# Token choice: the expert outputs turned by VectorE in 32 by 32 blocks, in place of a round trip through memory

## The chip, the cores and the metric

One NeuronCore of a Trainium2 chip runs the whole program. The metric is the device time of one execution in microseconds. The kernel before takes 2503.06 us, the median of 3 runs (2500.81 to 2505.09).

## The reference, cut to what matters

The program is four layers, each with a residual and a layer norm: window attention, token choice, linear attention, nested width attention. The change is in token choice (8 sequences of 1024 tokens of 256 numbers; tokens in groups of 16; 64 experts):

```python
grouped = x.reshape(x.shape[:-2] + (-1, ne, d))                    # groups of 16 tokens
logits = jnp.einsum('...btd,des->...btes', grouped, controller) + tie
perm = (logits == jnp.max(logits, axis=-3, keepdims=True))         # each expert takes one token of a group
sel = jnp.einsum('...btd,...btes->...besd', grouped, perm)
inner = jax.nn.relu(jnp.einsum('...besd,desf->...besf', sel, f1) + bias)
inter = jnp.einsum('...besf,esfd->...besd', inner, f2)             # the expert outputs
out = jnp.einsum('...besd,...btes->...btd', inter, perm)           # back to the tokens
x = layernorm(x + out)
```

## The kernel before, in words

`token_choice_layer` (from L820) handles two sequences, so 128 groups, in a block; there are NB = 4 blocks X = 0 to 3. The 64 experts are done in two halves of 32. A half has these stages:

- **selection**: for 8 pairs of tiles, PE transposes the one-hot choice (`pT`, L1254), ACT copies it (`chosen`, L1125), PE multiplies it with the tokens (`sel`, L1263), and the result is copied from PSUM half by ACT (L1153), half by DVE (L1188) into `sel`, as 32 experts by 128 groups.
- **h**: the first expert weights, two steps of 64 matmuls (L1269), with a relu into `hidden` by ACT (L1161) and DVE (L1194, 8 instructions a step).
- **inter**: the second expert weights, 8 steps of 8 matmuls (L1276). ACT (L1165) and DVE (L1199) copy the result into `wide`: partition = group, then 32 experts by 256 numbers. These are the expert outputs.
- **out**: back to the tokens, 4 steps of 16 matmuls (L1283), whose weights must have the partition run over 4 groups by 32 experts, which is not how `wide` stands after `inter`. DVE adds each result to `x` (L1209) and in the second half takes layer norm statistics (L176, L182).

Between `inter` and `out` the array is re-laid through memory: after each `inter` step SP stores 512 KB to `expert_outputs` (L1062, 8 a half), and the step `gather` loads the whole half back in four pieces of 1 MB in the other layout (L1076). `out` waits for its piece (`back`, L1244).

The order of all engines comes from one list `steps` (L856 to L863), each step with a block offset. The out steps of a half stand after the selection and the first `h` step of the next half, so the round trip has that time to hide in. The **early half** is `out` of half 0 of a block, behind the selection of half 1; on PE the transposes of the next block's tokens (`xT`, L957), their copies (L975) and `logits` (L969) follow it. The **late half** is `out` of half 1, behind the selection of the next block's half 0. After the last block nothing stands in front of it but the round trip; its end is called the **tail** here, with the linear attention layer's opening (weights loaded by ACT's queue, L1423 to L1429, once `wide` is free, and PE at L1549 and L1561). PSUM has four slots that steps use in turn, so `out` step 0 frees the slot of the fifth step after.

SP's queue carries the expert stores, the loads back, the next block's tokens (L1056), the second weights f2 (L1070) and the results (L1080), in the order of the list.

Of the kernel before, what the change touches and what calls it, by code (L numbers as in the profile page):

```python
# [819 lines left out]
def token_choice_layer(nc, block, semaphores, kept, x_in, y_out, controller, f1_in, f2_in, f1_bias, tie_in, ident_in, scratch):  # L820
# [35 lines left out]
    steps = [(-1, "gather", 1), (0, "f2", 2), (0, "f2", 3)] + s[2:] + e[:1] + late + [(-1, "aggregate", 0), (0, "spread", 1)]  # L856
    steps += e[1:4] + [(0, "f2", 4), (-1, "rescale", 0), e[4], (-1, "rescale", 1), e[5], (0, "f2", 5), (-1, "rescale", 2), e[6],
                       (-1, "rescale", 3), e[7], turned[0], e[8], turned[1], e[9]]
    steps += [(-1, "store", 1), (-1, "store", 0), (0, "gather", 0), (1, "load", 0), (1, "load", 1), (0, "f2", 6), (0, "f2", 7)]
    s, e, early = selection(1), experts(1), combination(0, 0)  # L860
    steps += s[2:] + e[:1] + early + [(1, "xT", n) for n in range(4)] + [(1, "logits", 0), (1, "second", 0)]
# [26 lines left out]
    def signal(name, per, step=1):  # L888
        return Signal(sem(name), per, step)
# [13 lines left out]
    left = [signal(f"left{half}", IN, 16) for half in range(2)]  # L903
    normed = [signal(f"normed{n}", NT) for n in range(2)]
    back = [signal(f"back{i}", 2, 16) for i in range(NC)]
# [71 lines left out]
    class First:  # L977
# [12 lines left out]
        def start_sp(self, sp):  # L990
            for s in (*f2_loaded, *x_loaded, *stored, *left, *back):
                s.start(sp)
# [49 lines left out]
    def programs(tail, sb, ps):  # L1042
        sel = sb("sel", [P, CH, EH, NG])
        schedule.slots = [ps(f"slot{i}", [P, 1024]) for i in range(4)]

        @block.sync
        def _(sp):
            def piece(step, X, seq, n, B):
# [8 lines left out]
                if kind == "inter":  # L1057
                    half, n = divmod(i, IN)
                    inter_even.wait(sp, X, i + 1)
                    alone(sp)  # L1060
                    inter_odd.wait(sp, X, i + 1)
                    left[half].by(sp.dma_start(scratch[half, :, 4 * n:4 * n + 4, :], wide[:, 4 * n:4 * n + 4, :]))  # L1062
# [54 lines left out]
        def _(act):  # L1117
# [9 lines left out]
            def piece(step, X, seq, n, B):  # L1127
# [42 lines left out]
        def _(dve):  # L1170
            def piece(step, X, seq, n, B):
# [11 lines left out]
                if kind == "sel":  # L1183
                    tp = i % TP
                    s = arrived(dve, X, step)[:, 512:1024].rearrange("p (g e) -> p e g", e=EH)
                    if tp == 0:
                        schedule.wait_filled(dve, X if i else X - 1, ("h", 1 if i else 3))
                    sel_odd.by(dve.tensor_copy(sel[:, 1, :, 16 * tp:16 * tp + 16], s))  # L1188
# [28 lines left out]
        def _(pe):  # L1217
# [6 lines left out]
            def piece(step, X, seq, n, B):  # L1224
# [18 lines left out]
                if kind == "out":  # L1243
                    back[i % NC].wait(pe, X, i // NC + 1)  # L1244
# [33 lines left out]
                if kind == "out":  # L1278
# [12 lines left out]
                    [(b.sem, b.count(NB - 1)) for b in back], schedule.left())  # L1291
# [834 lines left out]
def four_layers(nc, x, wq, wk, bq, bk, wv, bv, wo, bo, cos, sin, mask, maskT, ident, ident16,  # L2126
# [80 lines left out]
```

How the kernel before makes its waits and increments, by code:

```python
def wait_alone(eng, sem, value):  # L63
    eng.wait_ge(sem, value)
    alone(eng)
# [37 lines left out]
    def wait(self, eng, block, n=None):  # L103
        eng.wait_ge(self.sem, self.count(block, n))
# [27 lines left out]
    def wait_free(self, pe, b, key):  # L133
        old = self.before(key)
        if old is not None:
            for sem, per_sequence, position in self.emptied(old):
                pe.wait_ge(sem, b * per_sequence + position)
# [44 lines left out]
    def reciprocal_root(self, pool, b, use):  # L184
        pool.wait_ge(self.aggregated, self.count(b, use) * self.tiles)
        pool.tensor_scalar(self.mv[:, :, 1], self.mv[:, :, 1], LN_EPS, None, ALU.add).then_inc(self.var_ready, 1)
        pool.wait_ge(self.var_ready, self.count(b, use))
        pool.tensor_tensor(self.rstd[:, :], self.mv[:, :, 1], self.half[:, :], ALU.pow).then_inc(self.rstd_ready, 1)
# [45 lines left out]
    def wait_memsets(self, eng):  # L235
        eng.wait_ge(self.setup, 3)
# [15 lines left out]
def negative_mean(pool, ln, to, sems, X):  # L252
    pool.wait_ge(ln.rstd_ready, X + 1)
    pool.tensor_tensor(to[:, :], ln.mv[:, :, 0], ln.rstd[:, :], ALU.mult).then_inc(sems[0], 1)
    pool.wait_ge(sems[0], X + 1)
    pool.tensor_scalar(to[:, :], to[:, :], -1.0, None, ALU.mult).then_inc(sems[1], 1)
# [43 lines left out]
    def use(self, pe, X, step, B):  # L301
# [5 lines left out]
        if i > -4 * size:  # L307
            for sem, count in self.until(B + i // size, self.plan[i % size]):
                pe.wait_ge(sem, count)
        return self.slot_in(B, step)
# [649 lines left out]
    def logits(pe, X, s):  # L960
        if X == 0:
            pe.wait_ge(consts, 16 * NCONST)
        xT_even.wait(pe, X)
```

## Time and profile before

| | us |
|---|---|
| median of 3 runs | 2503.06 |
| lowest, highest | 2500.81, 2505.09 |
| the profiled execution's own time | 2499.96 |
| its span | 2498.1 |
| mean granted TensorE clock | 0.966 of full speed |
| busy: PE, DVE, ACT, POOL | 2175.6, 1420.4, 996.3, 901.0 |

The profiled execution is 3.1 us under the median of the runs. The token choice layer's matmuls run from about 1054 to 1438 us of the span. In the timelines a row is a start, a length, an engine, a line, an operation, out and in, and a count; in brackets stands the engine's idle time just before and what ended it.

### The profile page before, as it was taken

The numbers are of one execution on the slowest core, as the hardware profiler recorded it, in microseconds if no ns is written. First come the engines' busy times: TensorE is split into PE (matmuls) and PEld (weight loads), VectorE is DVE, ScalarE is ACT, GpSimd is POOL, SyncE is SP. The second block draws the span as 40 slices with busy tenths as digits, with TensorE's granted clock in tenths as the row PEclk, the third lists the DMA queues.
The fourth block names the chain that finished last, engine by engine and source line by source line (L and its number), as shares of the span: only waits on it lengthen the run. The fifth ranks groups of instructions, "written<-read, shape, count | busy, mean of one in ns | idle before, by whom it ended". The sixth has DMA issues, their size and how long they took to land.

```text
span 2498.1 us, 42625 instructions
## 1 busy us (share of the span) xinstructions
PE 2175.6 (87%) x17140; PEld 1362.6 (55%) x17140; DVE 1420.4 (57%) x2526; ACT 996.3 (40%) x1450; POOL 901.0 (36%) x573
## 2 busy tenths in 40 slices
PE   4899999999999999888878699999688888888885
PEld 2445555555555555566656556775455555555553
DVE  3545555555555555546566435544467777677772
ACT  1233333333333333444535243334245554555443
POOL 4222222222222220203123022101448877787784
PEclk7899999999999999999999899999789999999997
DMA  6555555555555554376796832101654465445511
GB/s 146 124 109 116 116 112 111 111 111 111 111 111 111 111 103 69 129 245 236 267 306 219 288 123 68 49 19 51 181 140 116 109 179 137 139 111 155 130 35 51
DMA packets 228355, 328.81 MB, mean 132 GB/s; under 512 B 14928, under 2 KB 167488, under 8 KB 227904
## 3 DMA queue, kind: packets, MB, share of 16 engines
q1 hardware_dynamic: 221168, 321.49, 49.2%
q10 hardware_dynamic: 6992, 4.60, 0.7%
q8 instruction: 137, 2.24, 0.4%
q14 instruction: 58, 0.48, 0.1%
HBM read 197.46 MB, written 127.93 MB: 130 GB/s over the span
## 4 chain that ended last, share of the span: by engine, by line
PE 57%; DVE 17%; DMA 7%; POOL 6%; ACT 6%; issue 3%; SPq 3%; ACTq 1%; DVEq 0%; POOLq 0%
PE l0a_slot L775 8%; PE l0a_slot L785 7%; PE l0a_O L710 6%; DVE l1f_rowmax L1978 5%; PE l1a_slot L1570 4%; PE l0a_slot L752 4%; POOL l1f_added L1855 3%; DMA l0f_wide<-expert_outputs 2%; PE l0a_slot L757 2%; ACT l0f_f L590 2%; PE l1a_slot L1561 2%; DMA expert_outputs<-l0f_wide 2%; PE l0a_slot L803 2%; DVE l0f_hidden L655 2%; PE l1a_slot L1612 2%
## 5 line engine op out<-in xcount | busy, mean ns | idle before, releaser
L590 ACT ACTIVATE l0f_f<-l0a_slot 128x1024 f32<-128x1024 f32 (+1 forms) x256 | 248.6, 972 | 339.0 <-PE l0a_slot L775 189.2
L655 DVE TENSOR_REDUCE l0f_hidden<-l0a_slot 128x4 f32<-128x1024 f32 (+1 forms) x256 | 293.5, 1156 | 114.2 <-PE l0a_slot L785 111.2
L1927 ACT ACTIVATE l1f_probs<-l1f_slot 128x1024 f32<-128x1024 f32 x240 | 244.1, 1023 | 251.0 <-PE l1f_slot L2109 245.7
L1978 DVE TENSOR_REDUCE l1f_rowmax<-l1f_slot 128x1 f32<-128x1024 f32 x240 | 287.5, 1217 | 70.1 <-PE l1f_slot L2100 69.7
L1855 POOL TENSOR_TENSOR l1f_added<-l1f_probs 128x1024 f32<-128x1024 f32 x117 | 277.4, 2371 | 133.1 <-ACT l1f_probs L1927 125.3
L775 PE MATMUL l0a_slot<-l0f_hidden 128*128 128x512 bf16 (+1 forms) x1024 | 296.0, 374 | 13.5 <-DMA l0f_hl<-qk_rows 9.1
L549 POOL TENSOR_TENSOR l0f_x<-l0f_x 128x512 f32<-128x512 f32 x32 | 40.8, 1274 | 538.6 <-DVE l0f_x L639 538.6
L2109 PE MATMUL l1f_slot<-l1f_Qs,l1f_Ks 128*128 128x256 f32 x960 | 171.5, 302 | 37.7 <-DVE l1f_lo L1968 14.8
L2100 PE MATMUL l1f_slot<-l1f_Ks,l1f_Qs 96*128 96x512 f32 x480 | 173.7, 447 | 26.0 <-DVE l1f_rowmax L1978 19.9
L2109 PEld LDWEIGHTS l1f_slot<-l1f_Qs,l1f_Ks 128*128 128x128 f32 x960 | 144.1, 194 | 93.1 <-DVE l1f_rowmax L1978 29.8
L710 PE MATMUL l0a_O<-l0f_f,l0f_wide 128*32 128x128 f32 x3840 | 156.1, 279 | 9.4 <-issue 9.4
L1857 POOL TENSOR_TENSOR l1f_added<-l1f_added 128x512 f32<-128x512 f32 x117 | 150.0, 1282 | 9.2
L2033 PE MATMUL l1f_os<-l1f_probs,l1f_V 128*32 128x256 f32 x1920 | 143.5, 392 | 0.1
L785 PE MATMUL l0a_slot<-l0a_Qs,l0f_hl 49*128 49x256 f32 (+1 forms) x1024 | 127.3, 327 | 18.3 <-ACT l0f_f L590 17.1
L785 PEld LDWEIGHTS l0a_slot<-l0f_hl,l0a_Qs 48*128 48x128 f32 x1024 | 77.7, 188 | 103.8 <-issue 103.8
L785 PEld LDWEIGHTS l0a_slot<-l0a_Qs,l0f_hl 49*128 49x128 f32 x1024 | 76.8, 186 | 103.4 <-issue 68.4
L785 PE MATMUL l0a_slot<-l0f_hl,l0a_Qs 48*128 48x256 f32 (+1 forms) x1024 | 128.7, 330 | 0.0
L752 PE MATMUL l0a_slot<-l0f_x,l0f_spread 128*128 128x512 f32 x256 | 123.1, 627 | 6.3 <-DVE l0f_spread L623 4.8
L710 PEld LDWEIGHTS l0a_O<-l0f_f,l0f_wide 128*32 128x32 f32 x3840 | 90.2, 109 | 63.3 <-issue 36.1
L775 PEld LDWEIGHTS l0a_slot<-l0f_hidden 128*128 128x128 bf16 x1024 | 63.8, 97 | 97.0 <-issue 62.3
L2100 PEld LDWEIGHTS l1f_slot<-l1f_Ks,l1f_Qs 96*128 96x128 f32 x480 | 76.9, 196 | 71.8 <-issue 30.9
L601 ACT COPY l0f_f<-l0a_O 128x512 f32<-128x512 f32 x64 | 37.5, 585 | 194.8 <-PE l0a_O L710 194.6
(194 smaller groups left out, 3750.3 us busy)
## 6 DMA issues: line engine op xcount, KB each, us to landing
expert_outputs<-l0f_wide SPq DMA_DIRECT2D x64, 512.0 KB, 5.3
l0f_wide<-expert_outputs SPq DMA_DIRECT2D x32, 1024.0 KB, 11.5
l1f_Ks<-kq_rows SPq DMA_DIRECT2D x48, 512.0 KB, 8.7
l0a_Qs<-qk_rows SPq DMA_DIRECT2D x90, 256.0 KB, 7.9
l0f_hl<-qk_rows SPq DMA_DIRECT2D x90, 256.0 KB, 14.9
qk_rows<-l0f_wide SPq DMA_DIRECT2D x32, 512.0 KB, 2.8
qk_rows<-l0f_x SPq DMA_DIRECT2D x32, 512.0 KB, 4.1
l0f_f<-in_dram SPq DMA_DIRECT2D x32, 512.0 KB, 7.7
```

Of the source, the lines that this page charges most:

```text
L590: exp_ready.by(act.activation(probs[:, t % 2, HG * g:HG * g + HG, 0:reach, :], s[:, :, 0:reach, :], ACT.Exp, scale=SCALE))
L655: max_ready.by(dve.reduce_max(rowmax[:, t, :, 2 * g:2 * g + 2], s[:, :, :, first:2 * P], AX))
L710: last = mm(O[t % 2][32 * j:32 * j + 32, g, :], V[:, tile - a, HG * g + j, :], probs[:, (t - a) % 2, HG * g + 2 * (j % 2) + j // 2, a, :], ...
L752: last = mm(s[:, BW * r:BW * r + BW], w[:, c, P * r:P * r + P], xT[:, n, c, :], start=c == 0, stop=c == CH - 1)
L775: at_end = mm(o[:, half, :, reach, :], ident16[:, :], table[:, reach, :].unsqueeze(1).broadcast_to([P, 2, wide, P]), start=not mask_ends, ...
L785: last = mm(o[:, half, j, reach, :].rearrange("p a q -> p (a q)"), left[r, 2 * g + j, here], right[r, 2 * g + j, moving], start=mask_ends ...
L1855: halved.by(pool.tensor_tensor(added[:, u, :], probs[:, 0, u, :], probs[:, 1, u, :], ALU.add))
L1857: add_done.by(pool.tensor_tensor(added[:, u, 0:SKT * QW], added[:, u, 0:SKT * QW], added[:, u, SKT * QW:HKT * QW], ALU.add))
L1927: exp_done.by(act.activation(probs[:, half, u - FIRST[b], :], s[:, :], ACT.Exp, scale=SCALE))
L1978: max_done.by(dve.reduce_max(rowmax[:, i:i + 1], s[:, :], AX))
L2100: last = mm(s[:, 512 * half:512 * half + 512], Qs[0:96, parity, u, P * t:P * t + P], Ks[0:96, parity, UNITS[u][0], 512 * half:512 * half + ...
L2109: last = mm(s[:, QW * j:QW * j + QW], Ks[:, parity, UNITS[u][0], P * kt:P * kt + P], Qs[:, parity, u, :], start=True, stop=True)
```

## The change

The stores of the expert outputs, the loads back and the scratch in memory go, with their semaphores `left` and `back`. In their place DVE turns `wide` in place: 8 instructions a half (`turn`, NTURN = 8), each over 128 partitions and 32 of the 256 columns by 32 experts; seen as partition, column, expert, every block of 32 partitions by 32 experts is transposed. An instruction reads and writes its 1024 numbers a partition with a step of 256 numbers, 1 KB. For the blocks to hold what `out` needs, the selection copies write the groups as (4 residues, 32 quads) and no longer as (32 quads, 4 residues): runs of 4 numbers where there were runs of 16. The turns are merged into the list among the selection steps of the next half. `out` waits for all 8 turns of its half. The linear attention layer's first loads wait for the last turn where they waited for the last load back.

```diff
+    NTURN = 8
+    def turns(offset, half):
+        return [(offset, "turn", NTURN * half + n) for n in range(NTURN)]
-    steps = [(-1, "gather", 1), (0, "f2", 2), (0, "f2", 3)] + s[2:] + e[:1] + late + [(-1, "aggregate", 0), (0, "spread", 1)]
+    steps = [(0, "f2", 2), (0, "f2", 3)] + merged(s[2:], turns(-1, 1)) + e[:1] + late + [(-1, "aggregate", 0), (0, "spread", 1)]
...
-    steps += [(-1, "store", 1), (-1, "store", 0), (0, "gather", 0), (1, "load", 0), (1, "load", 1), (0, "f2", 6), (0, "f2", 7)]
+    steps += [(-1, "store", 1), (-1, "store", 0), (1, "load", 0), (1, "load", 1), (0, "f2", 6), (0, "f2", 7)]
...
-    steps += s[2:] + e[:1] + early + [(1, "xT", n) for n in range(4)] + [(1, "logits", 0), (1, "second", 0)]
+    steps += merged(s[2:], turns(0, 0)) + e[:1] + early + [(1, "xT", n) for n in range(4)] + [(1, "logits", 0), (1, "second", 0)]
...
+        by_quad = sel[:, :, :, :].rearrange("p c e (j q) -> p c e j q", j=J)
+        by_word = wide[:, :, :].rearrange("p e d -> p d e")
-                if kind == "inter":
-                    left[half].by(sp.dma_start(scratch[half, :, 4 * n:4 * n + 4, :], wide[:, 4 * n:4 * n + 4, :]))
-                if kind == "gather":
-                    wait_alone(sp, left[i].sem, (X + 3) * IN * 16)
-                    rows = scratch[i, :, :, :].rearrange("(q j) e d -> (j e) q d", j=J)
-                    for n in range(NC):
-                        q = slice(NQ // NC * n, NQ // NC * (n + 1))
-                        back[n].by(sp.dma_start(wide[:, q, :], rows[:, q, :]))
-                    sel_odd.by(dve.tensor_copy(sel[:, 1, :, 16 * tp:16 * tp + 16], s))
+                    sel_odd.by(dve.tensor_copy(by_quad[:, 1, :, :, 4 * tp:4 * tp + 4], s))
+                if kind == "turn":
+                    half, n = divmod(i, NTURN)
+                    if n == 0:
+                        inter_even.wait(dve, X, IN * half + IN)
+                        inter_odd.wait(dve, X, IN * half + IN)
+                    part = by_word[:, D // NTURN * n:D // NTURN * (n + 1), :]
+                    turned_round.by(dve.transpose(part, part))
-                    back[i % NC].wait(pe, X, i // NC + 1)
+                    turned_round.wait(pe, X, NTURN * (i // NC + 1))
-                    [(b.sem, b.count(NB - 1)) for b in back], schedule.left())
+                    [(turned_round.sem, turned_round.count(NB - 1))], schedule.left())
```

On DVE, from the inter copies (`l0f_wide`) of half 0 to its late selection copies (`l0f_sel`), the order before:

```order
L1199 COPY l0f_wide<-l0f_slot 128x2x256 x2
L1194 TENSOR_SCALAR l0f_hidden<-l0f_slot,l0f_b 64x128 x8
L1199 COPY l0f_wide<-l0f_slot 128x2x256 x6
L1188 COPY l0f_sel<-l0f_slot 128x32x16 x8
L1194 TENSOR_SCALAR l0f_hidden<-l0f_slot,l0f_b 64x128 x8
```

At the same place now, down to the third selection copy:

```order
L1193 COPY l0f_wide<-l0f_slot 128x2x256 x2
L1188 TENSOR_SCALAR l0f_hidden<-l0f_slot,l0f_b 64x128 x8
L1193 COPY l0f_wide<-l0f_slot 128x2x256 x6
L1182 COPY l0f_sel<-l0f_slot 128x128x4
L1200 STREAM_TRANSPOSE l0f_wide<-l0f_wide 128x32x32
L1182 COPY l0f_sel<-l0f_slot 128x128x4
L1200 STREAM_TRANSPOSE l0f_wide<-l0f_wide 128x32x32 x2
L1182 COPY l0f_sel<-l0f_slot 128x128x4
```

Eight turns stand among the eight selection copies, one for one on the whole, and the last copy comes after the last turn.

On SP's queue, one half's stores and the steps behind them to the next block's tokens (`l0f_x<-x`), before:

```order
L1062 DMA expert_outputs<-l0f_wide 128x1024 x2
L1070 DMA l0f_f<-in_dram 128x4x256
L1062 DMA expert_outputs<-l0f_wide 128x1024 x4
L1080 DMA x<-l0f_x 128x8x256 x2
L1076 DMA l0f_wide<-expert_outputs 128x8x256 x4
L1056 DMA l0f_x<-x 128x8x256 x2
```

and now, from the weights (`l0f_f`) of a block on:

```order
L1062 DMA l0f_x<-x 128x8x256 x2
L1070 DMA l0f_f<-in_dram 128x4x256 x8
L1074 DMA x<-l0f_x 128x8x256 x2
L1062 DMA l0f_x<-x 128x8x256 x2
L1070 DMA l0f_f<-in_dram 128x4x256 x8
```

The loads of the next tokens stand right behind the stores of the block before.

## Rows read from the trace of the kernel before

**Rows 1.** The page: its head, and the chain that ended last by line.

```profile
span 2498.1 us, 42625 instructions
PE l0a_slot L775 8%; PE l0a_slot L785 7%; PE l0a_O L710 6%; DVE l1f_rowmax L1978 5%; PE l1a_slot L1570 4%; PE l0a_slot L752 4%; POOL l1f_added L1855 3%; DMA l0f_wide<-expert_outputs 2%; PE l0a_slot L757 2%; ACT l0f_f L590 2%; PE l1a_slot L1561 2%; DMA expert_outputs<-l0f_wide 2%; PE l0a_slot L803 2%; DVE l0f_hidden L655 2%; PE l1a_slot L1612 2%
```

**Rows 2.** Waits, 1054 to 1450 us: total us, times, longest us.

```profile
PE l0f_slot L1283 <- DMA l0f_wide<-expert_outputs: 43.2, 25, 12.2
PE l0f_slot L957 <- DMA l0f_x<-x: 6.7, 6, 1.2
```

**Rows 3.** Timeline of PE, the second block's early half.

```profile
1184.65 1.81 PE L1263 MATMUL l0f_slot<-l0f_chosen,l0f_hl 128*128 128x256 f32 x8
...
1186.44 1.20 PE L1263 MATMUL l0f_slot<-l0f_chosen,l0f_hl 128*128 128x256 f32 x8
...
1200.09 1.95 PE L1283 MATMUL l0f_slot<-l0f_wide,l0f_spread 128*64 128x256 f32 x16
1203.34 1.95 PE L1283 MATMUL l0f_slot<-l0f_wide,l0f_spread 128*64 128x256 f32 x16 [1.31 <-DMA l0f_wide<-expert_outputs]
...
1209.37 1.95 PE L1283 MATMUL l0f_slot<-l0f_wide,l0f_spread 128*64 128x256 f32 x16 [1.06 <-DMA l0f_wide<-expert_outputs]
1212.47 1.94 PE L957 MATMUL l0f_slot<-l0f_ident,l0f_x 128*128 128x128 f32 x16 [1.16 <-DMA l0f_x<-x]
...
1218.83 3.64 PE L969 MATMUL l0f_slot<-l0f_wide,l0f_ctrl 128*32 128x512 f32 x32 [1.41 <-DVE l0f_wide L975]
```

**Rows 4.** Timeline of SP's queue, there.

```profile
1191.70 8.50 SPq L1076 DMA_DIRECT2D l0f_wide<-expert_outputs  x4
1200.30 6.00 SPq L1056 DMA_DIRECT2D l0f_x<-x  x2
```

**Rows 5.** Timeline of DVE, the second block's late half.

```profile
1236.55 0.69 DVE L1188 COPY l0f_sel<-l0f_slot 128x512 f32<-128x512 f32 x1 [0.44 <-PE l0f_slot L1263]
...
1245.46 0.69 DVE L1188 COPY l0f_sel<-l0f_slot 128x512 f32<-128x512 f32 x1 [0.58 <-PE l0f_slot L1263]
1250.12 2.26 DVE L1194 TENSOR_SCALAR l0f_hidden<-l0f_slot,l0f_b 64x128 f32<-64x128 f32 x8 [3.96 <-PE l0f_slot L1269]
...
1253.81 1.40 DVE L176 BATCH_NORM_STATS2 l0f_ln_stats<-l0f_x 128x6 f32<-128x256 f32 x4
...
1265.92 1.17 DVE L182 BATCH_NORM_AGGREGATE l0f_ln_mv<-l0f_ln_stats 128x2 f32<-128x6 f32 x16
1267.00 1.26 DVE L1199 COPY l0f_wide<-l0f_slot 128x512 f32<-128x512 f32 x2
```

**Rows 6.** The chain that ended last, 1410 to 1480 us: start us, us, what.

```profile
1414.62 5.40 DMA expert_outputs<-l0f_wide
...
1435.97 0.38 ACTq L1423
...
1440.73 7.86 DMA l1a_head_blocks<-in_dram
...
1448.64 14.00 PE l1a_slot L1561 x32
```

**Rows 7.** Timeline of PE, the tail.

```profile
1442.15 5.27 PE L1549 MATMUL l1a_slot<-opening_ident,l1a_x 128*128 128x128 f32 x32 [4.37 <-issue]
```

**Rows 8.** Groups of DVE by shape: busy us, mean ns, idle before.

```profile
L1209 DVE TENSOR_TENSOR l0f_x<-l0f_slot,l0f_x 128x1024 f32<-128x1024 f32 x32 | 39.1, 1223 | 46.1 <-PE l0f_slot L1283 45.8
...
L195 DVE TENSOR_SCALAR l1a_y<-l1a_sum,l1a_ln_mv,l1a_ln_rstd 128x256 f32<-128x256 f32 x64 | 21.1, 406 | 0.0
...
L1959 DVE TENSOR_SCALAR l1f_xT<-l1f_slot,l1f_nw,l1f_nb 128x256 f32<-128x256 f32 x7 | 3.7, 535 | 0.0
```

**Rows 9.** Line L623 alone: duration ns least, median, most; first and last start.

```profile
L623 DVE COPY l0f_spread<-l0f_x x4: 361/367/6516, 8.7 to 15.7; 128x256 f32<-128x256 f32 x4
```

**Rows 10.** Stretches: length, engines' busy us, granted TensorE clock, DMA share, GB/s.

```profile
1235.00:1246.00 11.00, 10.36 (x80) 9.19 (x76) 6.07 (x9) 9.22 (x22) 0.68 (x1) 1.00 0.80 305
1263.00:1280.00 17.00, 14.98 (x135) 11.24 (x134) 14.31 (x45) 7.68 (x20) 12.10 (x12) 0.85 0.61 208
```

More of the change, by code:

```diff
@@ L817, in window_attention_layer, with token_choice_layer @@
                     spent=[(signal.sem, signal.step, signal.count(NBLOCK - 1)) for signal in spent])
-def token_choice_layer(nc, block, semaphores, kept, x_in, y_out, controller, f1_in, f2_in, f1_bias, tie_in, ident_in, scratch):
+def token_choice_layer(nc, block, semaphores, kept, x_in, y_out, controller, f1_in, f2_in, f1_bias, tie_in, ident_in):
     G = 16
@@ L902, in token_choice_layer @@
     inter_even = signal("inter_even", 2 * IN); inter_odd = signal("inter_odd", 2 * IN)
-    left = [signal(f"left{half}", IN, 16) for half in range(2)]
+    turned_round = signal("turned_round", 2 * NTURN)
     normed = [signal(f"normed{n}", NT) for n in range(2)]
-    back = [signal(f"back{i}", 2, 16) for i in range(NC)]
     summed = signal("summed", 2 * NC)
@@ L990, in start_sp @@
         def start_sp(self, sp):
-            for s in (*f2_loaded, *x_loaded, *stored, *left, *back):
+            for s in (*f2_loaded, *x_loaded, *stored):
                 s.start(sp)
@@ L1002, in start_dve @@
         def start_dve(self, dve):
-            for s in (xT_odd, rated, best_ready, choice_ready, lo_ready[0], normed[1], sel_odd, hidden_odd, inter_odd, summed):
+            for s in (xT_odd, rated, best_ready, choice_ready, lo_ready[0], normed[1], sel_odd, hidden_odd, inter_odd, turned_round, summed):
                 s.start(dve)
@@ L1056, in piece @@
                     x_loaded[i].by(sp.dma_start(x[:, X % 2, part, :], tokens(x_in, 2 * X + i)))
-                if kind == "inter":
[L1058 to L1061, printed above, removed]
-                    left[half].by(sp.dma_start(scratch[half, :, 4 * n:4 * n + 4, :], wide[:, 4 * n:4 * n + 4, :]))
                 if kind == "f2":
@@ L1149, in piece @@
                     tp = i % TP
-                    s = arrived(act, X, step)[:, 0:512].rearrange("p (g e) -> p e g", e=EH)
+                    s = arrived(act, X, step)[:, 0:512].rearrange("p (q j e) -> p e j q", q=4, j=J)
                     if tp == 0:
                         schedule.wait_filled(act, X if i else X - 1, ("h", 1 if i else 3))
-                    sel_even.by(act.copy(sel[:, 0, :, 16 * tp:16 * tp + 16], s))
+                    sel_even.by(act.copy(by_quad[:, 0, :, :, 4 * tp:4 * tp + 4], s))
                 if kind == "h":
@@ L1184, in piece @@
                     tp = i % TP
[L1185 removed]
+                    s = arrived(dve, X, step)[:, 512:1024].rearrange("p (q j e) -> p e j q", q=4, j=J)
                     if tp == 0:
                         schedule.wait_filled(dve, X if i else X - 1, ("h", 1 if i else 3))
[L1188 removed]
+                    sel_odd.by(dve.tensor_copy(by_quad[:, 1, :, :, 4 * tp:4 * tp + 4], s))
                 if kind == "h":
@@ L2137, in four_layers @@
             with ExitStack() as kept:
-                first, programs = token_choice_layer(nc, block, semaphores, kept, x1, x2, controller, f1, f2, f1_bias, tie, ident,
-                                                     dram("expert_outputs", (2, 128, 32, D)))
+                first, programs = token_choice_layer(nc, block, semaphores, kept, x1, x2, controller, f1, f2, f1_bias, tie, ident)
                 tail = window_attention_layer(nc, block, semaphores, x, x1, wq, wk, bq, bk, wv, bv, wo, bo, cos, sin, mask, maskT, ident,
```

## The prediction

> **What bounds the kernel now.** I read the page first: of a span of 2498.1 us the chain that ended last passes, with 2% each, through the stores of the expert outputs and through the loads back [rows 1]. So the round trip that the change removes is on the path. Next the waits inside the token choice layer: PE stood 43.2 us for pieces loaded back, in 25 waits, and 6.7 us for the next block's tokens [rows 2]. That is the most that can be won, 50 us, if what replaces the trip costs nothing. The timelines then tell what else fills those places.
>
> In the early half [rows 3], out steps that take PE 1.95 us start 3.0 us apart, each after a wait for its piece (1.31, then 1.06 twice), and the tokens come late too, since their loads stand on SP's queue behind the loads back, which took 8.5 us to issue [rows 4]. In the late half [rows 5] DVE paces the selection no more than PE does: eight copies of 0.69 us start 1.27 us apart (8.91 us from the first start to the last), so DVE is idle 0.58 us before each. That idle time, 8 x 0.58 = 4.6 us a half, is all the cover there is for the turns. Behind it DVE is the tighter engine: hidden 2.26 us, then adds with statistics, then the aggregate, and the inter copies start at 1267.00, without a pause.
>
> **What a turn costs.** No row shows a transpose by DVE, nor an instruction whose every number lies 1 KB from the last, on its input and its output. Bounds come from three rows.
> - Lower end: the add of 1024 numbers takes 1.223 us [rows 8] and the copy of 512 takes 0.69 [rows 5], so 1.04 ns a number and 0.16 us fixed. At that rate a turn takes 1.22 us. No row of DVE that reads 1024 numbers is below it.
> - A row with steps: L623 copies 256 numbers that lie 16 numbers apart, SBUF to SBUF, in 0.361 to 0.367 us; the one of 6.5 us is left aside, POOL was filling memory then [rows 9]. Such instructions go two numbers at a time: 256 numbers with two scalars take 535 ns from PSUM and 406 from SBUF, 129 ns less, which is half of 256 x 1.04 [rows 8]. Without steps L623 would take 128 x 1.04 + 160 = 0.29 us. It took (364 - 160) / 128 = 1.6 ns for each pair in place of 1.04. I read the 0.58 ns as the price of a read that never stays in place. A turn that pays it once a number takes 1024 x 1.62 + 160 = 1.82 us.
> - Upper end: the turn writes with the same step, and if the write pays as much on top, 1024 x 2.2 + 160 = 2.41 us.
>
> I take **2.0 us**, nearer to 1.82: the add of rows 8 reads two streams and writes one at the plain rate, so reads and writes run side by side and their prices should overlap in part.
>
> The Trainium skill (Vector Engine (DVE) Microarchitecture Reference, section 5.2, Measured stream behaviour on trn2) gives 1.73 ns a column for one input that hops at each element, 1.71 for an output that does, and 1.98 for all three streams. By it a turn would take an estimated 1.85 to 2.1 us, and the sum below would be 33 to 49 us before the clock's term. L623 agrees with its direction (1.6 ns); that the price falls on a transpose no run here shows.
>
> **The sum, by the length T of a turn.** Back to back, two copies of 0.69 take 1.26 us [rows 5], so each instruction overlaps the one before by about 0.1.
> - Selection, in the 7 halves that have one behind them (the tail has none): before, first copy to the end of the last 9.6 us. Now DVE alone sets it: 8 x (0.59 + T - 0.1) + 0.1 = 8T + 4.0. That is **8T - 5.6** longer. PE has its four slots ahead and ACT is not moved, so neither waits longer than DVE does; h, and out behind it, start later by that much.
> - Early half, blocks 0 to 2: from the first out to logits 18.74 us [rows 3]. Without the waits PE needs 4 x 1.95 + 2 x 1.94 + the 1.41 for the last token copy, 13.1. The tokens are no cause any more: their loads issue once the stores before them have landed, some 15 us before they are wanted. **5.6 won**, net 8T - 11.2, three times.
> - Early half, block 3: no tokens follow, so only the waits between outs go, 1.31 + 1.06 + 1.06 = **3.4**; net 8T - 9.0.
> - Late half, blocks 0 to 2: DVE's aggregate ended 16.97 us after hidden started [rows 5]. Without waits it is 2.26 + 4 x (1.23 + 1.40) + 1.17 = 13.95, DVE being the limit there and no longer the loads. **3.0 won**, net 8T - 8.6, three times.
> - Tail: from the last store to L1561 of the next layer 34.0 us [rows 6]. Now eight turns with nothing beside them, 8T - 0.8, then out 1.95, four adds and three statistics 9.1 until the slots are free, and 6.5 from L1549 to L1561 [rows 6, 7]: 8T + 16.8. The next layer's weights need 12.6 us from their first issue [rows 6] and may start at the last turn: hidden. Net **8T - 17.2**.
>
> Together 3(8T - 11.2) + (8T - 9.0) + 3(8T - 8.6) + (8T - 17.2) = **64T - 85.6**. It is zero at T = 1.34. At 1.22 it is -7.5, at 1.82 +31, at 2.0 **+42**, at 2.41 +69.
>
> Other edits: 64 MB of transfers less cost the engines nothing and the waits for them are counted. The selection copies write runs of 4 numbers where they wrote 16; runs of 16 ran at the plain rate (0.69 us), and I leave that, with the idle ACT as cover. The f2 loads issue earlier and nobody waited for them.
>
> TensorE's clock: the granted clock was 1.00 in 1235 to 1246 us, where PE was busy 10.4 of 11 us, and 0.85 in 1263 to 1280, where it waited between its steps [rows 10]; right after that a selection step took 1.81 us, and the next 1.20 [rows 3]. With a slower DVE, PE will have a gap at each selection step, and h behind it may start at the lower level (1.2 of 2.4 GHz). I put 0.6 us on each of 7 halves, **+4**.
>
> Sum +46.6 on the profiled execution's own 2499.96 us: 2546.6; that execution lies 3.1 us under the median of the runs, so I forecast **2550 us** for a median.
>
> **Rivals.**
> 1. **The turns run at the plain rate** (T = 1.22 to 1.30), and the kernel is faster or the same. The mechanism is the idle 0.58 us in front of each selection copy plus the waits removed behind it; the tail alone then gives 7. It decides below T = 1.34. For it: the copies from PSUM with a step of 32 numbers take 0.69 us, as those without [rows 5]. Against: those read PSUM, and the only stepped read of SBUF, L623, pays. -7.5 to -2.4, so 2496 to 2501. Chance 0.17. The Trainium skill (same page, section 3.8, The reshape front-end and per-opcode configuration) says that the transposing array is pipelined to one element a cycle a lane, which is this rival; it speaks of the array, not of the streams that feed it, and nothing in the trace before shows it.
> 2. **A part of the price** (T = 1.35 to 1.75): -1 to +26 before the clock, 2502 to 2533. Chance 0.08.
> 3. **Reads and writes both pay in full, or PE runs h at the lower clock.** T = 2.41 gives +69, with the clock +73: 2576. Or T = 2.0 and h at half speed in 7 halves: 7 x 3.7 (its length, within the 3.96 us that DVE waits for it [rows 5]) = +26 in place of +4: 2571. Both: 2598. Chance 0.18, of it 0.03 above 2592.
> 4. The change does not do what it says: were a piece of the trip left, PE would still wait for it; the order on SP's queue shows none left. No chance of its own.
>
> **How the numbers follow.** The forecast (T = 1.75 to 2.35, clock term 0 to 8) has 0.57. The range starts inside rival 2 at 2515 and ends at 2592: left out are rival 1 (0.17) and 0.03 above. What a measurement of this kernel can tell from no change is about 0.2%, 5 us. Faster by more than that: the lower part of rival 1 with the clock unchanged, 0.11. Within it: the rest of rival 1 (0.06) and the start of rival 2 (0.02), 0.08. Slower: 0.81.
>
> **What would show it.** In the profile after, the line of the transpose has 64 instructions with a mean near 2.0 us, so DVE gains some 125 us of busy time. In a selection stage DVE has no idle time, copies start about 2.5 us apart, and PE waits there for DVE's `l0f_sel`. Out steps start 1.95 us apart in the early half, no wait for a load stands in front of them, and logits come some 5 us later after the selection's start than before. From the last inter copy to L1561 it is about 33 us. DMA moves 64 MB less. The prediction is wrong if the transpose's mean is near 1.2 us, or if it is near 2 us and the sum is still near zero: then PE or the round trip, not DVE, set the selection.

## The result, and the profile after

The changed kernel takes 2560.22 us (median of 4 runs, 2555.83 to 2564.27), beside 2501.93 us of the kernel before on the same chip: ratio 1.0232, 95% interval 1.0211 to 1.0254. It is slower. The forecast was 2550 us in a range of 2515 to 2592. The profiled execution took 2559.29 us, 59.3 us more than that of before.

The page after: span, engines, transfers, and the chain by line, to be held against [rows 1].

```profile
span 2557.4 us, 42521 instructions
PE 2199.7 (86%) x17140; PEld 1393.3 (54%) x17140; DVE 1548.7 (61%) x2590; ACT 996.5 (39%) x1450; POOL 900.7 (35%) x573
DMA packets 185859, 261.69 MB, mean 102 GB/s; under 512 B 13392, under 2 KB 133184, under 8 KB 185408
PE l0a_slot L775 8%; PE l0a_slot L785 7%; PE l0a_O L710 5%; DVE l0f_wide L1200 5%; DVE l1f_rowmax L1979 5%; PE l1a_slot L1571 4%; PE l0a_slot L752 4%; POOL l1f_added L1856 3%; PE l0a_slot L757 2%; ACT l0f_f L590 2%; PE l1a_slot L1613 2%; PE l1a_slot L1562 2%; PE l0a_slot L803 2%; DVE l0f_hidden L655 2%; PE l0f_slot L1270 2%
```

Both pieces of the round trip are gone from the chain. The turns (L1200) stand in it with 5%, and h (L1270) has come in. DVE is busy 128.3 us more, PE 24.1 us more although it has the same matmuls. The transfers fell by 67.1 MB, from the 328.81 MB on the page of before.

The groups of DVE by shape (busy us, mean ns of one, idle before):

```profile
L1200 DVE STREAM_TRANSPOSE l0f_wide<-l0f_wide 128x1024 f32<-128x1024 f32 x64 | 141.4, 2232 | 0.2
...
L1182 DVE COPY l0f_sel<-l0f_slot 128x512 f32<-128x512 f32 x64 | 42.6, 667 | 10.8 <-PE l0f_slot L1264 10.8
```

A turn takes 2.23 us, between the 2.0 that the forecast took and its upper end of 2.41. The selection copies with their runs of 4 numbers cost nothing (0.67 us).

Waits of PE from 1054 to 1500 us (total, times, longest), against [rows 2]:

```profile
PE l0f_slot L1270 <- DVE l0f_sel L1182: 39.4, 8, 6.0
PE l0f_slot L1264 <- DVE l0f_sel L1182: 32.0, 15, 3.4
PE l0f_slot L1284 <- DVE l0f_wide L1200: 17.3, 1, 17.3
```

No wait for a load is left. PE now waits for DVE's selection copies, in front of h above all, and once, in the tail, for the turns.

Timelines of the second block's early half: DVE, then PE. The counterparts are [rows 5] for the copies (of the late half) and [rows 3] for PE.

```profile
1203.12 0.69 DVE L1182 COPY l0f_sel<-l0f_slot 128x512 f32<-128x512 f32 x1 [1.31 <-PE l0f_slot L1264]
1203.73 2.32 DVE L1200 STREAM_TRANSPOSE l0f_wide<-l0f_wide 128x1024 f32<-128x1024 f32 x1
1205.94 0.65 DVE L1182 COPY l0f_sel<-l0f_slot 128x512 f32<-128x512 f32 x1
...
1222.12 2.16 DVE L1200 STREAM_TRANSPOSE l0f_wide<-l0f_wide 128x1024 f32<-128x1024 f32 x1
1224.19 0.64 DVE L1182 COPY l0f_sel<-l0f_slot 128x512 f32<-128x512 f32 x1
1230.47 2.26 DVE L1188 TENSOR_SCALAR l0f_hidden<-l0f_slot,l0f_b 64x128 f32<-64x128 f32 x8 [5.64 <-PE l0f_slot L1270]
```

```profile
1211.51 2.04 PE L1264 MATMUL l0f_slot<-l0f_chosen,l0f_hl 128*128 128x256 f32 x8 [3.36 <-DVE l0f_sel L1182]
...
1225.03 5.40 PE L1270 MATMUL l0f_slot<-l0f_sel,l0f_f 128*64 128x128 f32 x64 [5.34 <-DVE l0f_sel L1182]
1230.25 7.09 PE L1284 MATMUL l0f_slot<-l0f_wide,l0f_spread 128*64 128x256 f32 x64
1237.27 3.71 PE L961 MATMUL l0f_slot<-l0f_ident,l0f_x 128*128 128x128 f32 x32
1242.39 3.64 PE L973 MATMUL l0f_slot<-l0f_wide,l0f_ctrl 128*32 128x512 f32 x32 [1.41 <-DVE l0f_wide L979]
```

From the first copy to the end of the last it is 21.7 us, without a gap on DVE behind the first copy. The last turn ends at 1224.28 and h starts at 1225.03, so no turn runs beside h. DVE stands still for 5.64 us while h runs. On PE the 64 matmuls of out follow each other without a wait, and from out to logits it is 12.1 us where it was 18.7. But h takes 5.40 us where the same 64 matmuls took 3.71 before. The next stretch (length, engines' busy us, granted clock, DMA share, GB/s), which begins just before h, shows why:

```profile
1224.00:1237.00 13.00, 11.97 (x128) 10.06 (x128) 6.70 (x13) 2.14 (x8) 0.00 (x0) 0.83 0.00 1
1475.00:1492.00 17.00, 0.00 (x0) 0.00 (x0) 16.89 (x9) 0.45 (x1) 0.00 (x0) 0.58 0.00 0
1492.00:1502.00 10.00, 9.85 (x64) 5.76 (x64) 5.86 (x12) 0.00 (x0) 0.00 (x0) 0.69 0.79 265
```

PE was busy nearly all of the 13 us at a granted clock of 0.83, a mean of the levels 1.2 and 2.4 GHz, behind a wait of 5.34 us. The tail shows it harder: 17 us without a matmul at 0.58, then out at 0.69, in 10.09 us where it took 7.09 in the middle.

The late half of the same block, DVE:

```profile
1281.50 0.64 DVE L1182 COPY l0f_sel<-l0f_slot 128x512 f32<-128x512 f32 x1
1288.13 2.26 DVE L1188 TENSOR_SCALAR l0f_hidden<-l0f_slot,l0f_b 64x128 f32<-64x128 f32 x8 [5.99 <-PE l0f_slot L1270]
...
1300.88 1.17 DVE L182 BATCH_NORM_AGGREGATE l0f_ln_mv<-l0f_ln_stats 128x2 f32<-128x6 f32 x16
```

From hidden to the end of the aggregate it is 13.92 us; the prediction had 13.95.

The chain that ended last, tail:

```profile
1474.86 0.70 DVE l0f_wide L1193
...
1475.66 0.30 DVE l0f_wide L1200
1475.96 1.78 issue
1477.74 14.36 DVE l0f_wide L1200 x7
...
1492.15 6.66 PE l0f_slot L1284 x32
...
1507.27 13.73 PE l1a_slot L1562 x32
```

On this chain 31.7 us lie between the end of the last inter copy (1475.56) and L1562, where before 34.0 us lay between the start of the last store's transfer and the same step [rows 6].

### The profile page after: what moved, and what is told of

It reads as the page before. It is cut to its first block, busy times and chain, and to the rows that moved or that the text cites. A ratio compares the mean times of both kernels' runs of the same rounds, so it can differ in the third digit from the quotient of the medians.

```text
span 2557.4 us, 42521 instructions
## 1 busy us (share of the span) xinstructions
PE 2199.7 (86%) x17140; PEld 1393.3 (54%) x17140; DVE 1548.7 (61%) x2590; ACT 996.5 (39%) x1450; POOL 900.7 (35%) x573
## 4 chain that ended last, share of the span: by engine, by line
PE 58%; DVE 24%; POOL 6%; ACT 5%; issue 3%; DMA 1%; ACTq 1%; SPq 0%; DVEq 0%; POOLq 0%
PE l0a_slot L775 8%; PE l0a_slot L785 7%; PE l0a_O L710 5%; DVE l0f_wide L1200 5%; DVE l1f_rowmax L1979 5%; PE l1a_slot L1571 4%; PE l0a_slot L752 4%; POOL l1f_added L1856 3%; PE l0a_slot L757 2%; ACT l0f_f L590 2%; PE l1a_slot L1613 2%; PE l1a_slot L1562 2%; PE l0a_slot L803 2%; DVE l0f_hidden L655 2%; PE l0f_slot L1270 2%
## 5 line engine op out<-in xcount | busy, mean ns | idle before, releaser
L775 PE MATMUL l0a_slot<-l0f_hidden 128*128 128x512 bf16 (+1 forms) x1024 | 296.1, 374 | 13.8 <-DMA l0f_hl<-qk_rows 9.4
L1200 DVE STREAM_TRANSPOSE l0f_wide<-l0f_wide 128x1024 f32<-128x1024 f32 x64 | 141.4, 2232 | 0.2
L1264 PE MATMUL l0f_slot<-l0f_chosen,l0f_hl 128*128 128x256 f32 x512 | 96.0, 346 | 37.3 <-DVE l0f_sel L1182 32.0
```

Of the source, the lines that this page charges most:

```text
L775: at_end = mm(o[:, half, :, reach, :], ident16[:, :], table[:, reach, :].unsqueeze(1).broadcast_to([P, 2, wide, P]), start=not mask_ends, ...
L1200: turned_round.by(dve.transpose(part, part))
```

## The experiments

**Theory**: the 1 KB step makes a turn nearly twice as long, and DVE, with turns and selection copies one for one, sets the selection; that outweighs the round trip, whose waits really were on the path. **Rivals**: the transpose is slow by itself; or the trip was hidden anyway and something else grew.

**1. plain_turn: the same turns on numbers that lie side by side.**

```diff
-                    part = by_word[:, D // NTURN * n:D // NTURN * (n + 1), :]
+                    part = wide[:, 4 * n:4 * n + 4, :].rearrange("p e (a b) -> p (e a) b", b=32)
```

> Each of the 64 turns transposes 1024 numbers that lie side by side (4 experts by 256 columns) in place, so the output isn't the reference's; count, size and waits are those of the change. Theory (the 1 KB step is the price of a turn): a turn takes 1.15 to 1.3 us, and by 64T - 85.6 the time comes to 2490 to 2500 us, 2510 at most if h still starts at the lower clock. Rival (the transpose is slow whatever its addresses): a turn stays near 2.2 us and the time near 2560 us.

Measured: 2493.14 us, ratio to before 0.9974 (0.9962 to 0.9986). The group of turns:

```profile
L1200 DVE STREAM_TRANSPOSE l0f_wide<-l0f_wide 128x1024 f32<-128x1024 f32 x64 | 77.1, 1222 | 0.2
```

The theory holds, and the rival falls: the transpose itself goes at the plain rate, and the step alone costs 1.0 us a turn and some 65 us in the whole (ratio to before 0.9974 in place of 1.0232). 64T - 85.6 gives -7.4 at T = 1.222; against the 2499.73 us of before in this set it was -6.6. That this fits so well is in part luck: h is long here too, in five of seven halves (5.07 to 6.49 us, 9.1 us over 3.71 together), and the sum has no term for it.

**2. short_turn: each turn cut to one of its 32 columns.**

```diff
-                    part = by_word[:, D // NTURN * n:D // NTURN * (n + 1), :]
+                    part = by_word[:, D // NTURN * n:D // NTURN * n + 1, :]
```

> Each turn transposes one column of 32 experts in place of 32 columns, so 31 of 32 columns are left unturned: the round trip is gone and nearly nothing is put in its place. Theory (the waits for the trip were worth what the sum gives them: 3 x 5.6 + 3.4 + 3 x 3.0, and 16 in the tail): 45 us less than before, 2452 to 2460 us, turns of 0.1 to 0.2 us, h back at 3.7 us. Rival (the waits come back elsewhere, the trip was mostly hidden): 2485 to 2502 us.

Measured: 2447.57 us, ratio 0.9791 (0.9770 to 0.9812), so 52 us less than before (2499.73), 7 us more than the 45 expected and past the lower end of its range. A shortened turn took 0.24 us where 0.1 to 0.2 was expected. The selection of the block's late half took 9.6 us as before, and h took 3.71 us in all 16 places. The round trip was on the path, and its removal is worth more than the sum gave it, although the 64 short turns are still there.

**3. hops: eight kinds of instruction over 1024 numbers in place of the eight turns.**

```diff
+                    turned_round.wait(dve, X, NTURN * half + n)
+                        turned_round.by(dve.transpose(plain, plain))
+                        turned_round.by(dve.transpose(plain, step))
+                        turned_round.by(dve.transpose(step, plain))
+                        turned_round.by(dve.transpose(step, step))
+                        turned_round.by(dve.transpose(two, two))
+                        turned_round.by(dve.transpose(eight, eight))
+                        turned_round.by(dve.tensor_copy(step, step))
+                        turned_round.by(dve.tensor_copy(plain, plain))
```

(The output stands first; `step` is 1 KB between numbers, `two` 8 B, `eight` 32 B. Each line stands under an `if n == 0` to `if n == 7`, left out here.)

> The eight turns of a half become eight different instructions over 1024 numbers, each behind a wait for the one before (the output isn't the reference's): 0 transpose side by side; 1 write 1 KB steps, read side by side is 2, read 1 KB steps and write side by side... in order: n=1 writes side by side in, steps out as given by the code (out plain, in stepped: n=1; out stepped, in plain: n=2); 3 both stepped as in the change; 4 both with steps of 8 B; 5 both with steps of 32 B; 6 a copy with 1 KB steps on both; 7 a copy side by side. Theory (each stepped stream has its own price and the two overlap in part): 0 at 1.2 us, 1 and 2 at 1.7 to 1.9, 3 at 2.2, 6 as 3. Rival a (only reads pay): 1 at 2.2, 2 at 1.2. Rival b (only writes pay): the reverse. Rival c (the transpose itself): 0 to 3 all near 2.2, 6 below 1.9. If the size of the step matters, 4 and 5 lie below 3; else they equal it.

Measured: 2509.76 us in its one execution; it was run for its durations. Each line alone, in the order of the diff (duration ns least, median, most; first and last start):

```profile
L1206 DVE STREAM_TRANSPOSE l0f_wide<-l0f_wide x8: 1235/1245/1247, 1088.7 to 1432.5; 128x1024 f32<-128x1024 f32 x8
L1208 DVE STREAM_TRANSPOSE l0f_wide<-l0f_wide x8: 1899/1958/2020, 1090.4 to 1433.8; 128x1024 f32<-128x1024 f32 x8
L1210 DVE STREAM_TRANSPOSE l0f_wide<-l0f_wide x8: 1900/1903/1909, 1092.4 to 1435.7; 128x1024 f32<-128x1024 f32 x8
L1212 DVE STREAM_TRANSPOSE l0f_wide<-l0f_wide x8: 2175/2250/2278, 1094.7 to 1437.7; 128x1024 f32<-128x1024 f32 x8
L1214 DVE STREAM_TRANSPOSE l0f_wide<-l0f_wide x8: 1223/1242/1262, 1097.5 to 1439.9; 128x1024 f32<-128x1024 f32 x8
L1216 DVE STREAM_TRANSPOSE l0f_wide<-l0f_wide x8: 2032/2116/2132, 1099.2 to 1441.2; 128x1024 f32<-128x1024 f32 x8
L1218 DVE COPY l0f_wide<-l0f_wide x8: 1189/1244/1273, 1101.8 to 1443.2; 128x1024 f32<-128x1024 f32 x8
L1220 DVE COPY l0f_wide<-l0f_wide x8: 658/682/705, 1103.5 to 1444.5; 128x1024 f32<-128x1024 f32 x8
```

Read and write each pay about the same when alone: (1958 - 1245) / 1024 = 0.70 ns a number for the read, 0.64 for the write. Together they pay 0.98, not 1.34: they run side by side in part. A step of 8 B costs nothing, one of 32 B nearly as much as 1 KB. The reads and writes alone came a little above the 1.7 to 1.9 us expected (1.96 and 1.90), and one expectation missed clearly: the copy with 1 KB steps took 1.24 us, 0.55 ns a number over the plain copy and far below the turn. Whether a copy, whose input and output steps are alike here, walks the addresses in the order written, no run tells.

**4. pe_fill: PE's gaps in the selection filled.** Half of the matmuls of a selection step are done twice.

```diff
-                            for part in (hi, lo):
+                            for part in (hi, lo) + ((hi, lo) if c == 0 and (X or i >= TP) else ()):
```

> The changed kernel with PE's idle time in the selections filled: 4 of the 8 matmuls of a selection step run twice (not in the very first selection). PE waits 2.0 us a step there less 0.6. Theory (h takes 5.2 to 6.1 us because PE had stood still in front of it and runs at the lower clock): h falls to 3.7 to 4.5 us and the time falls by 6 to 14 us, 2546 to 2554 us. Rival (the turns slow PE's reads, or the last wait of 5 us alone drops the clock): h stays at 5.2 to 6.1 us and the time is 2558 to 2565 us.

Measured: 2565.39 us (ratio to before 1.0255, 1.0227 to 1.0283), no better than the change. PE at h, two of seven halves:

```profile
1115.62 6.00 PE L1270 MATMUL l0f_slot<-l0f_sel,l0f_f 128*64 128x128 f32 x64 [5.07 <-DVE l0f_sel L1182]
...
1289.62 3.72 PE L1270 MATMUL l0f_slot<-l0f_sel,l0f_f 128*64 128x128 f32 x64 [3.71 <-DVE l0f_sel L1182]
```

A stretch inside each of these two (length, busy us of PE, PEld, DVE, ACT, POOL, granted clock, DMA share, GB/s):

```profile
1116.00:1121.00 5.00, 5.00 (x56) 5.00 (x54) 0.00 (x0) 0.00 (x0) 0.00 (x0) 0.57 0.01 3
1290.00:1293.00 3.00, 3.00 (x60) 3.00 (x58) 0.00 (x0) 0.00 (x0) 0.00 (x0) 1.00 0.02 5
```

So the clock makes h long, and not the turns' use of SBUF: in the slow stretch DVE does nothing at all, and PE goes through 56 matmuls in 5 us at 0.57 where it goes through 60 in 3 us at 1.00. Filling the gaps between the steps does not help. In six of seven halves one wait of 5.0 to 5.1 us stays in front of h, and h takes 5.1 to 6.5 us; only where that wait was 3.71 us did h take 3.72. The wait's length doesn't decide alone: plain_turn has an h of 3.71 us behind a wait of 3.09 us, columns_late one of 5.38 us behind 1.6 us. What decides in between, no run separates.

**5. late_two: the last two turns behind the last selection copy.**

```diff
-    merged(s[2:], turns(-1, 1)) + e[:1] + late
+    merged(s[2:], turns(-1, 1)[:6]) + turns(-1, 1)[6:] + e[:1] + late
```

(and the same in the early half.)

> The changed kernel with the last two of eight turns behind the last selection copy instead of among the copies. Theory (DVE alone sets the selection, and the 6 us for which it stands still while h runs are free cover): from the first selection copy to the last 17.7 us instead of 21.7, the two turns (4.4 us) lie beside h, the time falls by some 3.6 to 6 us in each of 7 halves, 2518 to 2535 us. Rival (the turns are only put off, out waits for them or the relu starts later by as much): 2552 to 2562 us.

Measured: 2525.58 us, ratio to before 1.0103 (1.0084 to 1.0122) in place of 1.0232, so some 32 us less than the change. DVE, the end of a late half:

```profile
1259.13 0.64 DVE L1182 COPY l0f_sel<-l0f_slot 128x512 f32<-128x512 f32 x1
1259.70 4.33 DVE L1200 STREAM_TRANSPOSE l0f_wide<-l0f_wide 128x1024 f32<-128x1024 f32 x2
1265.40 2.25 DVE L1188 TENSOR_SCALAR l0f_hidden<-l0f_slot,l0f_b 64x128 f32<-64x128 f32 x8 [1.37 <-PE l0f_slot L1270]
```

This selection began at 1242.01, so it took 17.8 us (expected 17.7). The two turns run in time in which DVE stood still. (h is still long in all seven halves, 5.0 to 5.4 us.) What costs is a turn **in front of a selection copy**, not a turn.

**6. act_sel: all selection copies on ACT.**

```diff
+                    s = slot[:, 512:1024].rearrange("p (q j e) -> p e j q", q=4, j=J)
+                    sel_odd.by(act.copy(by_quad[:, 1, :, :, 4 * tp:4 * tp + 4], s))
-                    sel_odd.by(dve.tensor_copy(by_quad[:, 1, :, :, 4 * tp:4 * tp + 4], s))
```

> The changed kernel with all selection copies on ACT, none on DVE. Theory (DVE's turns and copies together set the selection): 8 turns of 2.25 us alone, 17.5 to 18 us from the first turn, while ACT needs about 13.5 us; minus 4 us in each of 7 halves, plus some 3 us in the first selection, which has no turns: 2530 to 2540 us. Rival (PE, the slots or ACT set it as much as DVE): 2555 to 2570 us.

Measured: 2482.79 us, ratio 0.9939 (0.9923 to 0.9956): some 73 us less than the change by the ratios, and 15 us less than before (2498.04). The direction was expected, the size not. DVE and PE in the late half:

```profile
1226.49 17.29 DVE L1197 STREAM_TRANSPOSE l0f_wide<-l0f_wide 128x1024 f32<-128x1024 f32 x8
1243.81 2.26 DVE L1185 TENSOR_SCALAR l0f_hidden<-l0f_slot,l0f_b 64x128 f32<-64x128 f32 x8
```

```profile
1239.88 3.71 PE L1267 MATMUL l0f_slot<-l0f_sel,l0f_f 128*64 128x128 f32 x64 [1.32 <-ACT l0f_sel L1150]
1243.83 7.13 PE L1281 MATMUL l0f_slot<-l0f_wide,l0f_spread 128*64 128x256 f32 x64 [0.24 <-DVE l0f_wide L1197]
```

The expectation had still counted the turns into the selection. But h waits for the copies alone: it now starts 13.4 us after the first turn, runs beside the last turns at 3.71 us, and hidden and out follow the last turn at once. So the same 64 turns at nearly the same length (2270 ns in place of 2232) leave the kernel 58 us slower than before or 15 us faster, by what stands behind them on their engine. Of the 73 us between the two, 13.4 are h, which is short here.

**7 and 8. columns, columns_late: the array kept column by column**, the 32 experts of a column side by side; columns_late also puts three turns behind the last copy.

```diff
-        by_word = wide[:, :, :].rearrange("p e d -> p d e")
+        by_word = wide[:, :, :].rearrange("p e d -> p (e d)").rearrange("p (d e) -> p d e", e=EH)
+        by_expert = by_word.rearrange("p d e -> p e d")
-    act.copy(wide[:, e:e + 4:2, :], ...)
+    act.copy(by_expert[:, e:e + 4:2, :], ...)
```

(and likewise DVE's copy and out's `wide[:, q, :]`.)

> The array of the expert outputs is kept column by column, the 32 experts of a column side by side. The copies behind inter (ACT and DVE) write with steps of 128 B, the turns read and write side by side, out's matmuls read with steps of 128 B. Theory (a copy that works on one number at a time anyway pays nothing for a step, only the transpose does): copies stay at 0.69 us, turns at 1.22 us, and if PE's reads pay nothing either, the time is that of the side by side turns, 2488 to 2498 us. Rival (the price moves on to the copies or to out): each step of out twice as long would cost 7 us a half, 2545 to 2560 us; copies at 1.0 to 1.2 us would cost some 3 us a half, 2510 to 2520 us.

> As the run named columns, and the last three of eight turns behind the last selection copy. Theory: the selection takes 8 x 0.59 + 5 x 1.15 + 0.1 = 10.6 us, one more than without turns, and three turns (3.5 us) lie beside h: 7 us over the kernel with nothing in the trip's place in the halves, 8 us in the tail, 2458 to 2470 us. Rival (as for columns, out or the copies pay): 50 us more.

Measured: 2559.85 us (1.0254, 1.0236 to 1.0272) and 2534.10 us (1.0144, 1.0128 to 1.0159). Groups of columns:

```profile
L1201 DVE STREAM_TRANSPOSE l0f_wide<-l0f_wide 128x1024 f32<-128x1024 f32 x64 | 77.2, 1223 | 0.8 <-ACT l0f_wide L1160 0.7
L1194 DVE COPY l0f_wide<-l0f_slot 128x512 f32<-128x512 f32 x64 | 65.4, 1115 | 7.7 <-PE l0f_slot L1278 7.2
```

```profile
L1285 PE MATMUL l0f_slot<-l0f_wide,l0f_spread 128*64 128x256 f32 x466 | 114.9, 667 | 10.5 <-DVE l0f_wide L1201 10.5
```

The rival holds: the price moved. A copy that writes 128 B steps takes 1.115 us in place of 0.683 (ACT's 1.107 in place of 0.588), and a matmul of out that reads them 667 ns in place of 394.

**9 and 10. two_turned, four_turned: the kernel before with a part of the columns turned**, the others by the round trip; four_turned also has the selection copies on ACT.

```diff
+    NTURN = 2
+    SENT = slice(32 * NTURN, D)
-                        back[n].by(sp.dma_start(wide[:, q, :], rows[:, q, :]))
+                        for j in range(J):
+                            back[n].by(sp.dma_start(wide[EH * j:EH * j + EH, q, SENT], rows[j, :, q, SENT]))
```

> The kernel before, with two of eight turns among the selection copies (64 of 256 columns) and the other 192 columns by the round trip through memory; the loads back are 16 in place of 4, one for each j and piece, since the groups stand in the order of the change. Theory (DVE's idle 4.6 us in a selection are free cover for two turns of 2.25 us, and a quarter less to move shortens every wait for a piece): selection as before, 10 us at most; the waits for pieces fall from 43 us to some 20 us; 2470 to 2485 us. Rival (16 loads take longer to issue on SP's queue than 4, and the pieces come no earlier): 2495 to 2520 us.

> Four of eight turns, the other 128 columns by the round trip in 16 loads, and all selection copies on ACT. Theory: ACT sets the selection (13 us a half, 3 more than before), the four turns (9 us) lie beside it, half the bytes come back before out needs them, and the tail's trip is shorter by 5 to 8 us than before: 2465 to 2480 us, so better than act_sel (2483). Rival (the issue of the loads, not the bytes, sets the trip): waits for pieces stay near 40 us and the time is 2500 to 2520 us.

Measured: 2518.84 us (1.0069, 1.0053 to 1.0084) and 2484.71 us (0.9929, 0.9914 to 0.9944). Both expectations missed. Out's line in two_turned:

```profile
L1301 PE MATMUL l0f_slot<-l0f_wide,l0f_spread 128*64 128x256 f32 x512 | 72.5, 435 | 42.0 <-issue 30.1 <-DMA l0f_wide<-expert_outputs 11.9
```

With three quarters of the bytes out still stands 42.0 us, so fewer bytes, in more loads, won nothing there. ("issue" is idle time for which the profile shows no releaser.) SP's queue bears the rival out, beside [rows 4]:

```profile
1192.36 12.70 SPq L1086 DMA_DIRECT2D l0f_wide<-expert_outputs  x16
```

The 16 loads took 12.70 us to issue there, where the 4 took 8.50, and longer in each of the seven halves (8.9 to 13.8 us where it was 5.3 to 9.0). How much of the 42.0 us this makes, no run separates. The selection also grew, from 9.6 to 11.3 us: 4.6 us of idle time in eight pieces don't take two turns of 2.3 us for nothing. In four_turned the halves have no wait for a piece left, yet it ends level with act_sel. PE waits as long for ACT's selection work in both (27.8 and 27.9 us), and what four_turned saves in the tail (PE waits 9.2 us for the turns there, 17.3 in act_sel) it loses to waits of 4.0 and 1.0 us in front of the next layer, a slower out behind it and one long h.

**11. act_first: as act_sel, but DVE keeps the copies of the very first selection.**

```diff
-                    sel_odd.by(act.copy(by_quad[:, 1, :, :, 4 * tp:4 * tp + 4], s))
+                    if X or i >= TP:
+                        sel_odd.by(act.copy(by_quad[:, 1, :, :, 4 * tp:4 * tp + 4], s))
```

> As act_sel, but in the first selection, which has no turns, DVE keeps its eight copies. Theory (there ACT's 16 copies with 16 casts set the pace for nothing): 3 us less than act_sel, 2478 to 2481 us, ratio to before 0.991 to 0.994. Rival (the first selection waits for something else): as act_sel, 2483 us.

Measured: 2485.06 us (0.9932, 0.9918 to 0.9947). The rival holds: no gain. PE waited 2.54 us for a DVE copy there that act_sel does not wait for.

**12. pairs_late: as columns_late, but two columns side by side for each expert.**

```diff
+        by_pair = wide[:, :, :].rearrange("p e d -> p (e d)").rearrange("p (m e w) -> p m w e", e=EH, w=2)
+        by_expert = by_pair.rearrange("p m w e -> p e m w")
```

> As columns_late, but with two columns side by side for each expert: turns read and write with steps of 8 B, the copies behind inter write pairs of 8 B with 256 B between them, out's matmuls read such pairs. Theory (a hop is paid per access of up to two numbers): turns stay at 1.24 us, the copies' price above 0.68 us halves (0.9 us in place of 1.115) and out's matmul's above 394 ns goes or halves (394 to 530 ns in place of 660): 2460 to 2500 us. Rival (each number pays, pair or not): copies 1.1 us, out 660 ns, 2534 us as columns_late.

Measured: **2468.28 us**, ratio to before 0.9879 (0.9862 to 0.9895). Groups:

```profile
L1201 DVE STREAM_TRANSPOSE l0f_wide<-l0f_wide 128x1024 f32<-128x1024 f32 x64 | 76.5, 1221 | 0.2
L1194 DVE COPY l0f_wide<-l0f_slot 128x512 f32<-128x512 f32 x64 | 42.9, 700 | 10.6 <-PE l0f_slot L1278 10.1
```

```profile
L1285 PE MATMUL l0f_slot<-l0f_wide,l0f_spread 128*64 128x256 f32 x512 | 76.2, 459 | 10.1 <-DVE l0f_wide L1201 10.1
```

Pairs cost the copies almost nothing, the turns nothing, and out 65 ns a matmul. This version beats both kernels, the one before by 1.2%.

The Trainium skill (Vector Engine (DVE) Microarchitecture Reference, section 5.2, Measured stream behaviour on trn2) says that a stream goes at full rate only while it comes in runs of at least two adjacent words that start on an 8-byte boundary. The copies agree (700 against 683 ns, and 1115 for single words). The turns do not: with 8 B from number to number no two that follow each other are adjacent, and they took 1.24 us in hops and 1.22 here, the plain rate. There the measurement decides.

## Why the prediction was right, point by point

The direction and the path were right: the turns, and no longer the round trip, set the pace. The time fell inside the range, 10 us over the forecast, but two terms were too small, a turn's length by some 15 us and the clock's by some 9, and the waits won were larger than the sum by some 12, so the closeness is in part luck.

**The length of a turn** was the term that mattered, and it was mis-sized: 2.0 taken, 2.23 measured, inside the bounds 1.22 to 2.41, which makes 64 x 0.23 = 15 us. Two steps share it. The price of a read was taken from L623 as 0.58 ns a number, and hops has 0.70. And the write was given only some 0.18 ns on top ("their prices should overlap in part"), where hops has 0.98 together, so 0.28 on top. That they overlap in part was right: alone, read and write pay 1.34. The estimate drawn from the Trainium skill (Vector Engine (DVE) Microarchitecture Reference, section 5.2, Measured stream behaviour on trn2), 1.85 to 2.1 us, was low as well.

**The sum** follows the stretches with these lengths. In selections a turn took 2.25 us, in the tail 2.13 (the median there; each overlaps the one before by some 0.08, and all eight take 16.4 us). The terms, beside the change in the distance from the first h of a half to that of the next:

| stretch | terms, us | measured, us |
|---|---|---|
| block 0's second selection, 8T - 5.6 | 12.4 | 12.3 |
| three with an early half in front, each 8T - 11.2 | 6.8 | 6.9, 7.3, 7.3 |
| three with a late half in front, each 8T - 8.6 | 9.4 | 11.3, 10.5, 10.5 |
| block 3's early half (-3.4) and the tail (8T - 17.2) | -3.6 | -5.8 |

The measured column adds to some 60 us; the layer's first h came 1.8 us earlier, and the span grew by 59.3.

**The clock's term** was too small: 0.6 us a half was put on h, and h was longer by 13.4 us in 7 halves (5.17 to 6.11 us against 3.71). The total doesn't show it, since the waits won were larger than the sum had them. In the change it is 12.1 us from out to logits, not 13.1, mostly because out's 64 matmuls in a row take 7.09 us and not 4 x 1.95 = 7.8; and 31.7 us in the tail, where 8T + 16.8 gives 33.8. short_turn, where no selection is longer and h is short, shows their size by the same distances in its profile: 7.6, 6.9 and 6.4 us won where the sum had 5.6, 3.2, 4.9 and 4.2 where it had 3.0, and 24.6 where it had 3.4 and some 16, so some 12 us more in all. That this error and the clock's met is luck.

**The waits**: "PE waits there for DVE's `l0f_sel`", no wait for a load, the aggregate at 13.95, the selection at 8T + 4.0 (22.0 for 21.7) were right. "Now DVE alone sets it" was right of the time, but it took h to need the turns too: the prediction saw DVE's 3.96 us of rest while h runs [rows 5] and did not use it. act_sel and late_two show that only the copies behind the turns held h up.

**The rivals**: rival 1 (plain rate) is what plain_turn does, 2493 us where it said 2496 to 2501 (by difference -6.6, where it said -7.5 to -2.4), and the change does not. Rival 3's parts both came in, each about half: T 0.23 us above 2.0 where it had 0.41, and h longer by 13.4 us where it had 26.

## What to carry to other kernels

Before an off-path engine is given new work, ask what stands behind that work on its queue and who waits for it: with the same 64 instructions the kernel was 58 us slower than before while they stood in front of the copies that PE wanted, and 15 us faster once the copies were on another engine. Price a transpose by the steps of its two streams, and look for a layout in which pairs of words stay together; a layout that only moves single-word steps to the neighbours moves the price with them.

## What the runs showed that was not expected

- A step of 8 B is free for a turn (1.24 us), one of 32 B takes 2.12, one of 1 KB 2.25.
- A copy with 1 KB steps on both sides takes 1.24 us for 1024 numbers; a copy of 512 numbers from PSUM to 128 B steps takes 1.115.
- A matmul of 256 columns that reads numbers 128 B apart takes 667 ns, pairs 256 B apart 459, side by side 394.
- A turn takes 2.13 us in the tail, where PE stands still, and 2.25 in the selections. It is not the copies between them: in act_sel turns back to back take 2.25 us beside a working PE and 2.14 in the tail. Which work beside it costs the 0.1 us, no run tells.
